# One DRAM array for all early reads, a first half tile in two transfers, and dummy matmuls from a cleared tile

## The reference

```python
# layer 0: twice adj @ x, each through three dense layers with relu, then merged
ax = a @ x;  h = ax + (1.0 + eps[0]) * ax
for i in range(3): h = relu(h @ W[i].T + b[i])       # for x with W1, for x2 with W2
x = layernorm(x + concatenate((out1, out2), axis=1) @ Wm.T + bm)
# layer 1
A_hat = adj + eye;  d = rsqrt(sum(A_hat, axis=1))
x = layernorm(x + (d[:, None] * A_hat * d[None, :]) @ x @ W.T + b)
```

## Time and profile before

| what | value |
|---|---|
| time, median of 3 executions | 594.17 us (594.01 to 595.21) |
| profiled execution, its own time | 593.58 us |
| its span, first to last instruction | 591.8 us |
| TensorE busy | 584.8 us, 99% |
| VectorE busy | 540.5 us, 91% |
| ScalarE busy | 372.2 us, 63% |
| HBM read | 139.14 MB, 239 GB/s over the span |

### The profile page before, as it was taken

One profiled execution on the slowest core, in us unless ns is written; L12 is line 12 of the kernel. 1 busy time (PEld: TensorE's weight loads), 2 busy tenths in 40 slices (PEclk: granted clock), 3 DMA queues, 4 the chain that ended last, 5 costly groups with the idle time before them and its releaser, 6 DMA issues.

```text
span 591.8 us, 7721 instructions
## 1 busy us (share of the span) xinstructions
PE 584.8 (99%) x2676; PEld 484.3 (82%) x2676; DVE 540.5 (91%) x679; ACT 372.2 (63%) x494; POOL 28.7 (5%) x31
## 2 busy tenths in 40 slices
PE   8999999999999999999999999999999999999996
PEld 7888888888888888888888888867888888888885
DVE  6999999997988998998799999994899999989986
ACT  6554446842544773454667336486897888898893
POOL 1000000001100000110000020000200010010011
PEclk9999999999999999999999999999999999999998
DMA  9978565443554533354443375776699999999911
GB/s 334 370 271 296 202 226 197 142 148 137 214 205 170 190 145 142 142 213 174 181 150 138 138 293 189 286 299 212 245 353 413 364 370 383 400 365 374 387 42 71
DMA packets 27849, 141.56 MB, mean 239 GB/s; under 512 B 2608, under 2 KB 3376, under 8 KB 13616
## 3 DMA queue, kind: packets, MB, share of 16 engines
q1 hardware_dynamic: 27248, 139.54, 63.6%
q10 hardware_dynamic: 576, 1.70, 0.7%
HBM read 139.14 MB, written 2.10 MB: 239 GB/s over the span
## 4 chain that ended last, share of the span: by engine, by line
PE 98%; issue 0%; DVE 0%; POOL 0%; POOLq 0%; DVEq 0%
PE ps L468 81%; PE ps L544 7%; PE pd L486 6%; PE pd L497 2%; PE pd L530 1%; PE pd L592 1%; POOLq L118 0%; POOL rstd L1119 0%; DVE z L1090 0%; PE pd L494 0%; DVE stats L1095 0%; DVE outn L1104 0%; POOL identity L1123 0%; DVE mv L897 0%; DVEq L118 0%
## 5 line engine op out<-in xcount | busy, mean ns | idle before, releaser
L649 ACT ACTIVATE ahi<-raw 128x1024 fp32r<-128x1024 f32 x212 | 221.7, 1057 | 165.4 <-PE ps L468 152.8
L816 DVE TENSOR_TENSOR alo<-raw,ahi 128x1024 fp32r<-128x1024 f32 x212 | 257.2, 1220 | 29.7 <-ACT ahi L649 27.9
L468 PE MATMUL ps<-ahi,x2s 128*128 128x512 f32 x512 | 138.4, 389 | 0.0
L468 PE MATMUL ps<-ahi,x1hi 128*128 128x512 f32 x384 | 121.8, 393 | 0.0
L468 PE MATMUL ps<-alo,x1hi 128*128 128x512 f32 x384 | 120.5, 390 | 0.0
L468 PE MATMUL ps<-ahi,x1lo 128*128 128x512 f32 x384 | 120.4, 389 | 0.0
L468 PEld LDWEIGHTS ps<-ahi,x2s 128*128 128x128 f32 x512 | 96.1, 188 | 20.0
L468 PEld LDWEIGHTS ps<-ahi,x1hi 128*128 128x128 f32 x384 | 71.9, 188 | 15.9 <-issue 1.4
L468 PEld LDWEIGHTS ps<-alo,x1hi 128*128 128x128 f32 x384 | 72.0, 188 | 15.2 <-DVE alo L816 0.3
L468 PEld LDWEIGHTS ps<-ahi,x1lo 128*128 128x128 f32 x384 | 72.1, 188 | 14.9
L468 PE MATMUL ps<-alo,x2s 128*128 128x512 f32 x256 | 80.3, 389 | 0.0
(11 more groups left out here) (98 smaller groups left out, 510.7 us busy)
## 6 DMA issues: line engine op xcount, KB each, us to landing
raw<-a_t SPq DMA_DIRECT2D x108, 1024.0 KB, 4.9
raw<-a_t SPq DMA_DIRECT2D x32, 512.0 KB, 7.4
raw<-early SPq DMA_DIRECT2D x7, 512.0 KB, 7.8
xn<-x SPq DMA_DIRECT2D x3, 1024.0 KB, 8.1
out<-outn ACTq DMA_DIRECT2D x3, 512.0 KB, 6.7
par<-params SPq DMA_DIRECT2D x1, 708.0 KB, 12.8
raw<-head SPq DMA_DIRECT2D x2, 256.0 KB, 3.2
xn<-x SPq DMA_DIRECT2D x1, 512.0 KB, 7.2
```

The lines of the kernel that those rows point to most:

```text
L468: mm = pe.matmul(ps[bank + (CH * (q % 2) if layer else 0)][:, :], block_of(w, n), a[c], start=(n == 0 and k == 0), stop=(n == JB - 1 and k ...
L649: act.activation(ring_hi(layer, q, n), raw_tile(layer, n), ACT.Copy).then_inc(hi_ready, 1)
L816: dve.tensor_tensor(ring_lo(layer, q, n), raw_tile(layer, n), as_f32(ring_hi(layer, q, n)), ALU.subtract).then_inc(lo_ready, 1)
```

## The change

Everything that is read at the beginning lies in one DRAM array `lead`, in the order in which it is read: `x1` of piece 0, left and right quarter of tile 0, `x2` of piece 0, tile 0's second half, tile 1, piece 1, tiles 2 and 3, piece 2, tiles 4 to 7, pieces 3 to 5. The first half of tile 0 comes in two transfers of 128 partitions x 256 columns (`TW`), each with a semaphore, ScalarE rounds the two separately, and TensorE's first product is two matmuls of 256 columns. The order of the twelve products of tile 0 has all six of the first half ahead of the six of the second. On ScalarE the rounding of `x2` comes before that of the second half, on VectorE its subtraction comes before the second half's. The dummies are seven, on a tile `blank` that VectorE clears as its first instruction. Bytes, all other instructions and all buffers are the same.

```diff
-PE_WARM = 8
+PE_WARM = 7
...
-FIRST_TILE = [(0, 0, 0), (0, 0, 2), (0, 1, 0), (0, 1, 2), (0, 0, 1), (1, 0, 0),
-              (1, 1, 0), (1, 0, 1), (0, 1, 1), (1, 1, 1), (1, 0, 2), (1, 1, 2)]
+TILES_AHEAD = 2 * RAW
+
+LEAD = [("x1", 2 * P), ("left", TW), ("right", TW), ("x2", 2 * P), ("half", CW), ("tile1", QW), ("piece1", 4 * P),
+        ("tile2", QW), ("tile3", QW), ("piece2", 2 * (KB - 4) * P)]
+LEAD += [(f"tile{t}", QW) for t in range(4, TILES_AHEAD)] + [(f"piece{i}", 2 * QW) for i in range(3, 6)]
+LEAD_AT = {name: (P * sum(w for _, w in LEAD[:i]), w) for i, (name, w) in enumerate(LEAD)}
+FIRST_TILE = [(0, 0, 0), (0, 0, 2), (1, 0, 0), (0, 0, 1), (1, 0, 1), (0, 1, 0),
+              (0, 1, 2), (1, 0, 2), (1, 1, 0), (1, 1, 2), (0, 1, 1), (1, 1, 1)]
...
+        def lead_piece(name):
+            at, w = LEAD_AT[name]
+            return lead[at:at + P * w].rearrange("(p w) -> p w", p=P)
...
-            for c in range(CH):
-                sp.dma_start(raw[:, 0, 0, c * CW:(c + 1) * CW], head[c]).then_inc(half_in[c], 16)
-                if c == 0:
-                    sp.dma_start(xn[:, 1, k0 * P:k1 * P], x_piece(0)[1]).then_inc(x2_in, 16)
-            sp.dma_start(raw[:, 0, 1], early[0]).then_inc(raw_in[0], 16)
+            sp.dma_start(raw[:, 0, 0, 0:TW], lead_piece("left")).then_inc(quarter_in, 16)
+            sp.dma_start(raw[:, 0, 0, TW:CW], lead_piece("right")).then_inc(half_in[0], 16)
+            sp.dma_start(xn[:, 1, k0 * P:k1 * P], lead_piece("x2")).then_inc(x2_in, 16)
+            sp.dma_start(raw[:, 0, 0, CW:], lead_piece("half")).then_inc(half_in[1], 16)
+            sp.dma_start(raw[:, 0, 1], lead_piece("tile1")).then_inc(raw_in[0], 16)
             load_x(1)
             for p in range(1, RAW):
-                sp.dma_start(raw[:, p, 0], early[2 * p - 1]).then_inc(even_in[p], 16)
-                sp.dma_start(raw[:, p, 1], early[2 * p]).then_inc(raw_in[p], 16)
+                sp.dma_start(raw[:, p, 0], lead_piece(f"tile{2 * p}")).then_inc(even_in[p], 16)
+                sp.dma_start(raw[:, p, 1], lead_piece(f"tile{2 * p + 1}")).then_inc(raw_in[p], 16)
...
+                    if first and k + bank == 0:
+                        pe.wait_ge(x1_rounded, 1)
+                        for t, done in enumerate((hi_quarter, hi_half)):
+                            pe.wait_ge(done, 1)
+                            pe.matmul(ps[0][:, t * TW:(t + 1) * TW], block_of(w, 0), a[0][:, t * TW:(t + 1) * TW],
+                                      start=(t == 0), stop=False, skip_group_check=True)
+                        continue
...
-            pe.wait_ge(warm_ready, 1)
+            pe.wait_ge(blank_ready, 1)
             for k in range(PE_WARM):
-                pe.matmul(pd[:, 3, 0:P], identity[:, :], identity[:, :], start=True, stop=True)
+                pe.matmul(pd[:, 3, 0:P], blank[:, :], blank[:, :], start=True, stop=True)
...
                         for c in range(CH):
+                            if n == 0 and c == 0:
+                                for t, landed, done in ((0, quarter_in, hi_quarter), (1, half_in[0], hi_half)):
+                                    act.wait_ge(landed, 16)
+                                    act.activation(ahi[:, 0, t * TW:(t + 1) * TW], raw[:, 0, 0, t * TW:(t + 1) * TW],
+                                                   ACT.Copy).then_inc(done, 1)
+                                round_x(0, (1,))
+                                continue
...
-                        if n == 0:
-                            round_x(0, (1,))
                         return
...
-            act.dma_start(xn[:, 0, k0 * P:k1 * P], x_piece(0)[0]).then_inc(x_in[0], 16)
+            act.dma_start(xn[:, 0, k0 * P:k1 * P], lead_piece("x1")).then_inc(x_in[0], 16)
...
-                    if n == 0:
-                        split_x(0, (1,))
+                        if n + c == 0:
+                            split_x(0, (1,))
                     return
...
+            dve.memset(blank[:, :], 0.0).then_inc(blank_ready, 1)
             _, k0, k1 = X_PIECES[0]
             dve.wait_ge(x_in[0], 16)
```

More of the change, by code:

```diff
@@ L107 @@
 X_PIECE_AT = {KB * q + k: i for i, (q, k, _) in enumerate(X_PIECES)}
-X_PIECE_START = [2 * P * P * sum(k1 - k0 for _, k0, k1 in X_PIECES[:i]) for i in range(len(X_PIECES))]
-FIRST_TILE = [(0, 0, 0), (0, 0, 2), (0, 1, 0), (0, 1, 2), (0, 0, 1), (1, 0, 0),
-              (1, 1, 0), (1, 0, 1), (0, 1, 1), (1, 1, 1), (1, 0, 2), (1, 1, 2)]
+TILES_AHEAD = 2 * RAW
[5 more added lines that the diff above has]
+              (0, 1, 2), (1, 0, 2), (1, 1, 0), (1, 1, 2), (0, 1, 1), (1, 1, 1)]
 SECOND_TILE = [(b, c, k) for c in range(CH) for b in range(2) for k in (0, 2)]
@@ L114, with build @@
 X_AFTER = {1: 1, 3: 2, 6: 3, 12: 4, 20: 5}
-def build(nc, a_t, head, early, x12, params, out):
+def build(nc, a_t, lead, params, out):
     with ExitStack() as ctx:
@@ L159, in build @@
         identity = sb("identity", [P, P])
+        blank = sb("blank", [P, P])
         halves = sb("halves", [P, KB])
@@ L183, in build @@
         x2_in = sem("x2_in")
+        quarter_in = sem("quarter_in")
+        hi_quarter = sem("hi_quarter")
         x1_rounded = sem("x1_rounded")
@@ L239, in build @@
         warm_ready = sem("warm_ready")
+        blank_ready = sem("blank_ready")
         gain_ready = sem("gain_ready")
@@ L248, in x_piece @@
             _, k0, k1 = X_PIECES[i]
[L249 to L252, removed]
+            return lead_piece(f"piece{i}").rearrange("p (t w) -> p t w", t=2)
+        def lead_piece(name):
+            at, w = LEAD_AT[name]
+            return lead[at:at + P * w].rearrange("(p w) -> p w", p=P)
         def wait(eng, s, value):
@@ L468, in products @@
                     mm = pe.matmul(ps[bank + (CH * (q % 2) if layer else 0)][:, :], block_of(w, n), a[c],
-                                   start=(n == 0 and k == 0), stop=(n == JB - 1 and k == 1))
+                                   start=(n == 0 and k == 0), stop=(n == JB - 1 and k == 1),
+                                   skip_group_check=isinstance(q, int) and layer + q == 0)
                     if n == JB - 1 and k == 1 and (b, c) != banks[-1]:
@@ L1172 @@
     ], axis=1))
-    head = np.ascontiguousarray(a_t[0][:, 0].reshape(P, CH, CW).transpose(1, 0, 2))
-    early = np.ascontiguousarray(a_t[:RAW].transpose(0, 2, 1, 3).reshape(2 * RAW, P, QW)[1:])
+    tiles = a_t[:RAW].transpose(0, 2, 1, 3).reshape(TILES_AHEAD, P, QW)
     x12 = np.stack([x["x"].reshape(QUARTERS, P, QW), x["L0_gnn_x2"].reshape(QUARTERS, P, QW)], axis=2)
+    parts = {"left": tiles[0][:, 0:TW], "right": tiles[0][:, TW:CW], "half": tiles[0][:, CW:]}
+    parts.update({f"tile{t}": tiles[t] for t in range(1, TILES_AHEAD)})
+    parts.update({f"piece{i}": x12[q][:, :, k0 * P:k1 * P] for i, (q, k0, k1) in enumerate(X_PIECES)})
+    parts["x1"], parts["x2"] = parts["piece0"][:, 0], parts["piece0"][:, 1]
     arrays = {
         "a_t": a_t,
-        "head": head,
-        "early": early,
-        "x12": np.concatenate([(x12[q].transpose(1, 0, 2) if i == 0 else x12[q])[:, :, k0 * P:k1 * P].reshape(-1)
-                               for i, (q, k0, k1) in enumerate(X_PIECES)]),
+        "lead": np.concatenate([parts[name].reshape(-1) for name, _ in LEAD]),
         "params": params,
```

## The result

| | before | after |
|---|---|---|
| time, median (22 executions each, side by side) | 594.56 us (593.83 to 596.65) | 595.73 us (594.79 to 598.43) |
| ratio, 95% interval | | 1.0022 (1.0014 to 1.0030) |
| profiled execution, its own time and span | 593.58 and 591.8 us | 596.50 and 594.7 us |

The change makes the kernel slower by 1.2 us; its interval, 0.14 to 0.30%, lies on both sides of the 0.2% that were taken for the edge of what can be told. One execution of g3 (3403.54 us) and one of the kernel before beside the last group (1538.2 us) lie far from all others and are left out of the ratios. The forecast was 593.9 with 592.9 to 594.8; the measured time lies 0.9 us above that range.

What follows compares the result with a forecast made beforehand. VectorE's chain from tile 1's landing to tile 7 was taken to bound the end: -0.83 at the first tile, +0.08 at tile 2, +0.75 at tile 7, about 0, 593.6; the middle to 594.2 gave 593.9 us, range 592.9 to 594.8.

Steps and rivals of the forecast that it cites:

- The landings: Early transfers: bytes ahead set each landing at 382 GB/s; `x2`, second half and tile 1 stay about 4.2, 4.92, 6.47.
- the extra issue on SP: SP's queue: the added transfer delays every later issue by about 0.46 us, taken to cost nothing at the end.
- its cover: Tile 1's transfer: it waits behind the bytes ahead until 4.4 to 5.1, hiding the later issue; otherwise 0.46 us.
- rival 4: Tile 1's landing: the 0.46 us on each issue shows there and reaches the end, 594.4 us; chance 0.06.
- split the difference: End time: between 593.6 from the profiled execution and 594.2 from the timed median, the middle was taken, 593.9 us.
- rival 3: TensorE's start: cleared-tile dummies don't raise the clock, which rises late, at 7.5 say: +0.55, 594.5 us; chance 0.10.
- a cover for a low clock: Tile 0 on TensorE: holes up to 5.66 hide what a low clock loses up to about 4.9.
- the one with low `x1`: Tile 0 on TensorE: the product that needs `x1`'s low part, ready after 0.43 us more of VectorE, at 4.5.
- The 0.9 us of an earlier first product: TensorE's start: first matmul at 4.05 instead of 4.96, the gain absorbed by tile 7, about 0 at the end.
- VectorE's chain from tile 1's landing: Tile 1 to tile 7: VectorE runs unbroken from 7.13 to `alo` at 26.20 and decides the end; chance 0.62.
- 0.75 us to spare: Tile 7 on TensorE: it arrives 0.75 us earlier and waits for VectorE's `alo`, so that much delay is absorbed.
- The rule on batching transfers: Start-up transfers: advice to batch to 1 MiB and more, not borne out by this trace; if it held, rival 4 results.

Runs made afterwards that it cites:

- g3: The kernel before with the new order of tile 0's products, roundings and subtractions alone; transfers, arrays and dummies as before: ratio 1.0003, 594.93 us.
- the last group: Two kernels: the kernel before with `x2` on ScalarE's queue, new order, ten blank dummies, with and without 1 KB pieces: ratios 0.9991 and 0.9990.
- h1: The kernel before with its first transfer cut into left and right quarter on one semaphore, ScalarE waiting once: ratio 1.0026, 595.93 us.
- i2: The kernel before with `x2` issued on ScalarE's queue, so SP issues all behind it 0.46 us earlier: ratio 0.9988, 594.17 us.
- i1: The kernel before with its first transfer cut in two, the right quarter issued on ScalarE's queue: ratio 1.0024, 596.65 us.
- i5: The changed kernel with the right quarter issued on ScalarE's queue behind `x`, all else as changed: ratio 1.0004 to the kernel before, 594.86 us.
- e3: The kernel before with only the dummies changed, seven on the cleared tile instead of eight on `identity`: ratio 1.0008, 595.25 us.
- g4: The kernel before with ten dummies on the cleared tile instead of eight on `identity`: ratio 0.9997, 594.54 us.
- h4: The kernel before with the new order of tile 0 and ten dummies on the cleared tile: ratio 0.9998, 594.67 us.
- e1: The changed kernel with its early reads in three arrays again; split, order and dummies as changed: ratio 1.0015 to the kernel before, 595.58 us.
- g1: The kernel before with its first transfer cut into quarters, ScalarE waiting for two semaphores and rounding the half at once: ratio 1.0030, 596.50 us.
- e4: The changed kernel with fourteen dummies instead of seven: ratio 1.0006 to the kernel before, 595.25 us.
- h2: The kernel before with its first transfer cut by partitions into two of 128 KB, pieces of 2 KB as before: ratio 1.0021, 595.80 us.
- h3: The kernel before with its first transfer still one of 256 KB, but made of 256 pieces of 1 KB: ratio 0.9985, 594.31 us.
- i3: The kernel before with one more wait on SP behind its first issue, later issues 0.22 to 0.30 us late: ratio 1.0009, 595.23 us.

## Why the prediction was wrong

**The landings: the step that failed.** It took the transfers behind the first for byte-bound, at 382 GB/s, and therefore left `x2`, the second half and tile 1 where they were, at 4.2, 4.92 and 6.47. They came at 5.3, 7.1 and 8.35. The price of the extra issue on SP was taken at nothing, and at 0.46 us if its cover was gone (rival 4, chance 0.06). The cut with the later issues that go with it cost 0.26% in h1, 1.5 us by the ratio and 1.3 by the medians, about three times that bound. The bound was made from the issue's own duration; no row of the kernel before showed what the engines do with one transfer more, and the range should have been wider for it. The premise itself, engines full at 382 GB/s, was open to doubt from the rows, since rows 4 have 412 GB/s for 7.10 to 26.25; in i2, with one issue fewer on SP, 413 were moved from 3 to 5 us. The late landings went through VectorE to the end: it began tile 1 1.90 us later, stood 0.46 us more for piece 1 of `x`, and had tile 7's `alo` at 28.79 instead of 26.20. Which property of the cut makes the landings late stays open between i1 and i5.

**One execution was read as the kernel.** Rows 5 gave 6.47 for tile 1. Four other kernels with the same transfers (e3, g3, g4, h4) had it at 7.10, 7.76, 7.28 and 6.61 in their profiles; the mean of these five, the kernel before among them, is 7.0. The eight with the cut have 7.49 to 8.99, mean 8.2. So the cut moves the head of the deciding chain by 1.1 us in the mean, and the kernel before was predicted from its best sight. The prediction noticed that the profiled execution was 0.6 us below the median, gave a late clock and the DMA's side as the two possible causes, and then split the difference.

**The clock: a part that is small, and two events.** Rival 3 had the clock rise late. In the changed kernel's profile it rose early enough (where no hole lies between, the products from 5.79 on start 0.23 to 0.34 us apart) and then fell back, from 8.67 to 12.08, behind the holes that the late transfers had torn. The prediction had named holes up to 5.66 and called them a cover for a low clock, not a danger to a high one. Low executions go with the cut: 19 of 89 in the seven kernels that have it and no more than the old number of dummies, 2 of 287 in all others without it. Six of 22 executions of the change are low, 596.07 to 598.43 us; the median of the other 16 is 595.4, still 0.9 above the kernel before. So of the 1.17 us about 0.3 are the falls, as a rough estimate and about what the profiled execution gave; the rest goes with the late landings, and isn't separated further.

The late rise of rival 3 does occur, though: until about 9.6 in e1, which is the change but for the array, where it put TensorE 0.75 us behind VectorE, and until 13.1 in g1, where it was 2.4 us. Two executions of the change took 597.70 and 597.75 us at a mean clock of 0.998; whether that is a late rise no profile shows, and the column "low" can't. The reason that rival 3 gave, that zeros in the dummies do not raise the clock, is not borne out: in e4 it was up when the first products came, 0.23 us apart, and in g1 it rose late behind `identity`.

**What held.** The dummies ran from 1.05 to 4.06 (forecast 1.0 to 4.0), the first product started at 4.06 (4.05), the one with low `x1` at 4.67 (4.5): the terms for what lies ahead of the cut's consequences were right. The 0.9 us of an earlier first product brought nothing, as said: VectorE's chain from tile 1's landing decides at tile 7, in eleven of the twenty profiled executions. The statement that TensorE would have 0.75 us to spare there was wrong in the profiled execution only because the clock's fall made TensorE the later one, 29.12 against VectorE's 28.79.

The rule on batching transfers (the Trainium skill, DMA: Bandwidth & Descriptors, Bandwidth) was set aside because 382 GB/s were moved with small transfers in flight. h1 and h2 side with the rule in the outcome, 157 and 217 GB/s; i5, with the same small transfers and 1.0004, does not in the time. That it would be the length of the pieces, h3 excludes.

## What to carry to other kernels

Before work is put on making the first instruction of the busiest engine earlier, follow the chain that ends last at the first place where that engine waits; here it began at the landing of tile 1, and what delayed that transfer was paid in full. Where two engines meet, compare when each gets there: the holes and the low clock on TensorE added up to the whole loss, and yet most of it would have stayed without the low clock, since VectorE was nearly as late. A start-up transfer that is cut in two buys an earlier first piece and can make everything behind it later: count the issues on the queue ahead of the deciding transfer, and rather move one to another queue (in i2 0.12% gained by the ratio, 0.06% by the medians). A forecast of a few tenths of a per cent about the start needs several profiled executions, since one landing differed by 1.3 us between kernels with the same transfers.

## What the runs showed of the hardware

- One transfer more at the start, of the same bytes, with the issues behind it 0.46 us later, cost 0.21 to 0.26% (1.2 to 1.5 us), whether cut by columns or by partitions (h1, h2); on the other queue, with no issue of SP later, 0.24% in i1, but only 0.04% in the changed kernel (i5). In h1 and h2 the DMA engines moved 157 and 217 GB/s from 3 to 5 us where the uncut kernels before and e3 moved 383 and 390:

```profile
3.00:5.00 2.00, 2.00 (x11) 2.00 (x10) 0.57 (x3) 0.63 (x1) 0.99 (x6) 1.00 0.67 217
```
```profile
3.00:5.00 2.00, 1.50 (x8) 1.23 (x7) 0.63 (x2) 0.63 (x1) 0.99 (x6) 1.00 1.16 390
```

- TensorE's clock fell to 1.2 GHz in the changed kernel behind holes of 1.1 and 1.6 us with products in between, and in i1 behind one of 2.5 us from start to start. It didn't fall behind one of 1.7 us in e4 (6.84 to 8.55) and one of 1.8 in i3 (5.09 to 6.90), so the length of a hole alone doesn't tell. With fourteen dummies in place of seven there was no low execution, 0 of 11 against 6 of 22.
- When the clock first rises differs by many microseconds: about 5.0 us in the kernel before, 9.6 in e1, 13.1 in g1, each in one profiled execution. The granted clock reads 1.00 from the span's start although the dummies run at 1.2 GHz: 333 ns for a weight load, against 192 later. Spacing and durations tell the rise, the granted clock only the fall.
- In g1, with two waits ahead of the first activation, the activation table was loaded behind the first of them (3.94 instead of 1.19 us), and its 1.28 us delayed the first rounding; in the kernels with one wait there it was loaded at 1.16 to 1.70, beside the transfer.
